# A two-layer gated block on one core: keys and values of the first cross-attention as one-pass products of high and low parts, the context transposed two steps sooner, loads in halves, the first statistics early

## What is computed

```python
ln = layer_norm(layernorm(x), gamma_l, beta_l)      # 112 latents for each of 8 batches
xn = layer_norm(ctx, gamma_x, beta_x)               # 375 context rows
q  = (ln @ Wq)                                      # 8 heads of 64
k_x, v_x = split(xn @ Wkv); k_l, v_l = split(ln @ Wkv)
k  = concat(rope(k_x), k_l); v = concat(v_x, v_l)   # 487 keys and values
x  = x + tanh(g) * (softmax(q k^T / 8) v) @ Wo
...                                                 # experts (top 2 of 8, and a shared one), then the
...                                                 # second layer's attention and expert attention
```

## Time and profile before

| | |
|---|---|
| median of 3 runs | 807.23 us (804.37 to 810.54) |
| profiled execution | 806.53 us |
| its span, first to last instruction | 804.7 us |
| TensorE / VectorE / ScalarE / GpSimd busy | 93% / 55% / 46% / 23% |
| mean granted TensorE clock | 0.994 of full speed |
| the stage in question | from the start to about 268 us |

### The profile page before, as it was taken

How to read it: one execution, slowest core, us unless ns; L and a number is a source line. 1 busy time by engine, 2 the same in 40 slices (tenths; PEclk the granted TensorE clock), 3 DMA queues, 4 the chain that set the end, 5 groups by cost and what they waited for, 6 DMA issues and landing times.

```text
span 804.7 us, 14480 instructions
## 1 busy us (share of the span) xinstructions
PE 752.2 (93%) x5152; PEld 553.4 (69%) x5152; DVE 446.2 (55%) x1136; ACT 371.8 (46%) x991; POOL 182.4 (23%) x301
## 2 busy tenths in 40 slices
PE   3889999999999999999999999998999988999998
PEld 1355555555564666698889888666676767889976
DVE  1657758667666331122122221857788788698741
ACT  2456656556565621132332232467787878211210
POOL 2212112112100026000000001754446535411000
PEclk9999999999999999899999999999999999999999
DMA  4422224233121394155645542260000000000001
GB/s 137 113 56 60 73 78 149 68 113 83 36 55 38 94 353 179 61 173 212 228 163 175 187 139 84 73 220 2 2 2 2 2 2 2 1 1 1 0 12 35
DMA packets 43451, 69.74 MB, mean 87 GB/s; under 512 B 6531, under 2 KB 34956, under 8 KB 43124
## 3 DMA queue, kind: packets, MB, share of 16 engines
q1 hardware_dynamic: 41844, 65.14, 25.4%
q0 software_dynamic: 1536, 3.67, 1.5%
HBM read 52.56 MB, written 8.26 MB: 76 GB/s over the span
## 4 chain that ended last, share of the span: by engine, by line
PE 73%; DVE 9%; DMA 6%; ACT 5%; issue 4%; POOL 2%; SPq 1%; ACTq 0%; DVEq 0%
PE ps L1362 10%; PE ps L1595 7%; PE ps L1607 7%; PE ps L1813 7%; PE ps L1406 6%; PE ps L1409 6%; DMA OT<-slot_rows 4%; PE ps L1526 4%; PE ps L1850 3%; PE ps L1448 3%; PE ps L1695 3%; PE ps L1515 3%; PE ps L1468 3%; PE ps L1396 2%; PE ps L1419 2%
## 5 line engine op out<-in xcount | busy, mean ns | idle before, releaser
L1362 PE MATMUL ps<-ident,arena 112*122 112x112 f32 (+5 forms) x584 | 82.9, 276 | 21.2 <-ACT arena L576 13.7
L732 ACT ACTIVATE OT<-ps,bt 128x128 f32<-128x128 f32 x168 | 47.9, 368 | 114.2 <-PE ps L1595 113.3
L1362 PEld LDWEIGHTS ps<-ident,arena 112*122 112x122 f32 (+5 forms) x584 | 63.8, 155 | 46.1 <-issue 27.7
L1595 PE MATMUL ps<-OT,arena 128*128 128x128 f32 x672 | 80.5, 279 | 0.2 <-DVE OT L1076 0.2
L1595 PEld LDWEIGHTS ps<-OT,arena 128*128 128x128 f32 x672 | 78.7, 196 | 0.6 <-issue 0.6
L927 DVE TENSOR_REDUCE negmax<-ps 112x1 f32<-112x375 f32 x128 | 61.1, 539 | 30.4 <-PE ps L1695 30.3
L1813 PE MATMUL ps<-arena_r 128*112 128x384 f32 x384 | 75.9, 346 | 1.9 <-DVE acc L1164 1.0
L1607 PE MATMUL ps<-arena,OT 128*128 128x256 f32 x336 | 75.8, 379 | 0.0
L922 DVE TENSOR_REDUCE negmax<-ps 112x1 f32<-112x487 f32 x64 | 39.4, 657 | 56.8 <-PE ps L1448 56.6
L1090 DVE COPY yo<-ps 128x256 f32<-128x256 f32 x21 | 8.9, 424 | 108.3 <-PE ps L1607 108.3
L1607 PEld LDWEIGHTS ps<-arena,OT 128*128 128x128 f32 x336 | 62.3, 190 | 7.6
(11 more groups left out here) (269 smaller groups left out, 1373.6 us busy)
## 6 DMA issues: line engine op xcount, KB each, us to landing
arena<-in_up_w SPq DMA_DIRECT2D x21, 1024.0 KB, 5.1
arena<-in_down_w SPq DMA_DIRECT2D x8, 1024.0 KB, 11.9
arena<-arena SPq DMA_DIRECT2D x128, 60.9 KB, 2.0
arena<-in_wqkv SPq DMA_DIRECT2D x1, 3072.0 KB, 10.4
arena<-in_ctx SPq DMA_DIRECT2D x8, 375.0 KB
slot_rows<-acc SPq DMA_DIRECT2D x3, 896.0 KB, 5.0
OT<-slot_rows SPq DMA_DIRECT2D x21, 128.0 KB, 5.0
slot_out<-yo SPq DMA_DIRECT2D x21, 128.0 KB, 1.7
```

The lines of the kernel that those rows point to most:

```text
L732: act.activation(he[:, i % 2, m, :], ps[:, 2 * (i % 2) + m // 4, (m % 4) * SLOT:(m % 4 + 1) * SLOT], ACT.Gelu, bias=bt[:, i % 3, m:m + 1]) ...
L1362: return pe.transpose(dst, src, ident[0:k, 0:k])
L1595: ins = pe.matmul(ps[:, 2 * (i % 2) + m // 4, (m % 4) * SLOT:(m % 4 + 1) * SLOT], wu[i % 3][:, c, m * P:(m + 1) * P], xgT[:, i % 2, c, :], ...
```

## The change

Six things, in the order of the diff's importance:

1. For batches 1 to 7 ScalarE makes `kv_hi`, the high part of `kvin` (`kv_high`, 128 x 976 elements, at the head of step 2 of the batch before), and VectorE `kv_lo` (`kv_low`, behind the two maxima of that step). The weights `wkv` are split once: `wkv_hi` by ScalarE ahead of the first keys (128 x 2048), `wkv_lo` by VectorE in two halves of 1024 at the ends of steps 0 and 1 of batch 0. `l0_kv` then makes each piece of six fp32r products in place of two fp32 ones (four records); TensorE waits for `kv_lo` first. Batch 0 stays in fp32. The two buffers are single.
2. `l0_t1` of batch n+1 moves from step 2 to step 0 (step 1 for n = 0), on TensorE behind the scores, on ScalarE ahead of the exponentials; `l0_q` moves from step 2 to the end of step 1. `ctx_hat(n + 2)` moves from step 3 to step 2. `L0_SEQ` follows.
3. The context of batch 1 is loaded ahead of the first swap; its statistics, and those of latents 1, are made before the first rotation; `hat` of batch 1 is made between the first two copies of keys. From then on the latents' statistics run two batches ahead in place of one.
4. The clearing DMAs of the experts' slots go in six halves of 448 KB in place of three of 896 KB; the shared expert's weights in four halves of 512 KB in place of two of 1024 KB; two loads of second-layer weights start two swaps later.
5. GpSimd's order follows VectorE's.
6. The arena grows by 256 columns (1 KB for each partition).

```diff
+        (kv_hi, kv_lo, wkv_hi, wkv_lo) = layout(21760, [P, KC, NKP0], [P, KC, NKP0], [P, KC, 1024], [P, KC, 1024], of=arena_r)
...
             sp.dma_start(x[:, 1, :], a["x"][1, :, :]).then_inc(s_x, 16)
+            ctx_load(1, cx, 1)
...
-                sp.dma_start(xs[k * B * TQ:(k + 1) * B * TQ, :].rearrange("(t p) d -> p t d", p=TQ), acc[:, :, :])\
+                half = B * TQ // 2
+                sp.dma_start(xs[k * half:(k + 1) * half, :].rearrange("(t p) d -> p t d", p=TQ), acc[:, 0:B // 2, :])\
...
-                    if i == 0:
-                        ctx_load(1, cx, 1)
...
-                    if i in (11, 15, 19):
-                        clear_slots(i // 4 - 2)
-                    if i == 14:
-                        sp.dma_start(sw_u, a["sw_up"].rearrange("(c p) n -> p c n", p=P)).then_inc(s_shw, 16)
-                    if i == 18:
-                        sp.dma_start(sw_d, a["sw_down"].rearrange("(m p) n -> p m n", p=P)).then_inc(s_shw, 16)
-                    if i == 22:
+                    if i in (11, 15, 16, 20, 22, 23):
+                        clear_slots((11, 15, 16, 20, 22, 23).index(i))
+                    if i in (12, 14):
+                        c = (12, 14).index(i)
+                        sp.dma_start(sw_u[:, c], a["sw_up"][c * P:(c + 1) * P, :]).then_inc(s_shw, 16)
+                    if i in (18, 19):
+                        m4 = (18, 19).index(i) * 4
+                        sp.dma_start(sw_d[:, m4:m4 + 4], a["sw_down"][m4 * P:(m4 + 4) * P, :]
+                                     .rearrange("(m p) n -> p m n", p=P)).then_inc(s_shw, 16)
+                    if i == 24:
...
-                    if c == 0 and n >= 2:
-                        act.wait_ge(L0["v"], (n - 1) * 4)
+                    if c == 0 and n == 2:
+                        act.wait_ge(L0["v"], 4)
+                    elif c == 0 and n > 2:
+                        act.wait_ge(s_kvlo, n)
...
+            def kv_high(n):
+                if n >= 2:
+                    act.wait_ge(L0["v"], 4 * n)
+                act.wait_ge(L0["t1e"], (n + 1) * KC)
+                act.activation(kv_hi, kvin[n % 2], ACT.Copy).then_inc(s_kvhi, 1)
...
+                if n + 1 < B and u == (n == 0):
+                    l0_t1(n + 1, q)
+                if n + 1 < B and u == 2:
+                    kv_high(n + 1)
                 l0_exp(n, 2 * u)
                 if u == 2:
-                    if n + 1 < B:
-                        l0_t1(n + 1, q)
...
-                    if u == 2:
-                        l0_q(n + 1, q)
...
+                if n + 1 < B and u == 1:
+                    l0_q(n + 1, q)
...
-                if n == 0 and u == 1:
-                    ctx_hat(1, 1)
-                if n + 2 < B and u == 3:
+                if n + 2 < B and u == 2:
                     ctx_hat(n + 2, p)
...
+            act.wait_ge(s_w0, 16)
+            act.activation(wkv_hi, wkv, ACT.Copy).then_inc(s_kvhi, 1)
             l0_k(0, 0)
             l0_q(0, 0)
             l0_v(0, 0, 0)
+            ctx_hat(1, 1)
...
+            dve.wait_ge(s_x, 16)
+            latents_stats(1, x, 0)
+            ctx_stats(1, 1)
+            latents_stats(1, xn, 1)
...
+            def kv_low(n):
+                if n >= 2:
+                    dve.wait_ge(L0["v"], 4 * n)
+                dve.wait_ge(s_kvhi, n + 1)
+                dve.tensor_tensor(kv_lo, kvin[n % 2], kv_hi.bitcast(F32), ALU.subtract).then_inc(s_kvlo, 1)
+
+            def w_low0(c):
+                dve.wait_ge(s_kvhi, 1)
+                dve.tensor_tensor(wkv_lo[:, c, :], wkv[:, c, :], wkv_hi[:, c, :].bitcast(F32), ALU.subtract)\
+                   .then_inc(s_kvlo, 1)
...
+                if n + 1 < B and u == 2:
+                    kv_low(n + 1)
+                if n + 2 < B and u == (2 if n == 0 else 0):
...
+                    latents_norm(1)
+                if n + 2 < B and u == (2 if n == 0 else 0):
+                    latents_norm(n + 2)
+                if n == 0 and u < 2:
+                    w_low0(u)
...
             def l0_kv(n, p, j, kinds=("k", "v")):
-                pe.wait_ge(L0["t1e"], (n + 1) * KC)
+                if n:
+                    pe.wait_ge(s_kvlo, 2 + n)
+                else:
+                    pe.wait_ge(L0["t1e"], KC)
                 for kind in kinds:
                     bank = l0_bank_free(kind, n, j)
                     for c in range(KC):
-                        if kind == "k":
+                        first, last = c == 0, c == KC - 1
+                        if n == 0 and kind == "k":
                             ins = pe.matmul(ps[:, bank, 0:NK0], wkv[:, c, j * P:(j + 1) * P], kvin[p][:, c, 0:NK0],
-                                            start=(c == 0), stop=(c == KC - 1))
+                                            start=first, stop=last)
+                        elif n == 0:
+                            ins = pe.matmul(ps[0:KP0, bank, :], kvin[p][:, c, j * KP0:(j + 1) * KP0],
+                                            wkv[:, c, 512:1024], start=first, stop=last)
                         else:
-                            ins = pe.matmul(ps[0:KP0, bank, :], kvin[p][:, c, j * KP0:(j + 1) * KP0],
-                                            wkv[:, c, 512:1024], start=(c == 0), stop=(c == KC - 1))
+                            for k, (wv, xv) in enumerate(((wkv_hi, kv_hi), (wkv_hi, kv_lo), (wkv_lo, kv_hi))):
+                                if kind == "k":
+                                    ins = pe.matmul(ps[:, bank, 0:NKP0], wv[:, c, j * P:(j + 1) * P], xv[:, c, :],
+                                                    start=first and k == 0, stop=last and k == 2)
+                                else:
+                                    ins = pe.matmul(ps[0:KP0, bank, :], xv[:, c, j * KP0:(j + 1) * KP0],
+                                                    wv[:, c, 512:1024], start=first and k == 0, stop=last and k == 2)
                     ins.then_inc(L0[kind], 1)
...
-                if u == 2 and n + 1 < B:
+                if n + 1 < B and u == (n == 0):
                     l0_t1(n + 1, q)
...
-                elif n + 1 < B:
-                    if u == 2:
-                        l0_q(n + 1, q)
+                if n >= 2 and u == 1:
+                    l0_x(n - 2)
+                if n + 1 < B and u == 1:
+                    l0_q(n + 1, q)
                 if n >= 2 and u == 2:
                     l0_r(n - 2)
                 if u >= 2 and n + 1 < B:
                     l0_kv(n + 1, q, u - 2)
-                if n >= 2 and u == 1:
-                    l0_x(n - 2)
 
...
+    def context(n):
+        return ("t1", n, 0), ("t1", n, 1)
 
     def pair(n, j):
         return ("k", n, j), ("v", n, j)
 
-    seq.extend(prelude() + pair(0, 1))
+    seq.extend(context(0) + (("k", 0, 0), ("q", 0, 0), ("v", 0, 0)) + pair(0, 1))
     for n in range(B):
-        seq.extend(pair(n, 2) + pair(n, 3))
+        if 0 < n < B - 1:
+            seq.extend(context(n + 1))
+        seq.extend(pair(n, 2))
+        if n == 0:
+            seq.extend(context(1))
+        seq.extend(pair(n, 3))
         if n >= 2:
             seq.append(("x", n - 2, 0))
         if n + 1 < B:
-            seq.extend(begin(n + 1))
+            seq.append(("q", n + 1, 0))
         if n >= 2:
             seq.append(("r", n - 2, 0))
         if n + 1 < B:
```

39 lines of the change are left out of this document (17 added, 22 removed).

## The result

The changed kernel takes **786.31 us** (median of four, 783.97 to 788.33) against 806.51 beside it (median of four, 804.37 to 810.54): a ratio of 0.975, 95% interval 0.9714 to 0.9785. The prediction said 782, in a range of 774 to 791. The profiled execution took 783.97 us, its span is 782.2; that of before took 806.5 with a span of 804.7. Two traces further down, of the changed kernel again and of the whole loads, are of executions 1.5% and more above the fastest run of their kernel, and their experts' loops count in no mean.

What follows compares the result with a forecast made beforehand. The first stage was taken as bound by TensorE's own pieces plus a little waiting. Terms 18.8 + 1.5 + 5.0 = 25.3 us off the profiled 806.5 gave 781.2, so 782 us as median, range 774 to 791.

Steps and rivals of the forecast that it cites:

- keys and values, 28 pairs: First stage, batches 1 to 7: six fp32r products replace four fp32 records; a pair 2.70 us against 3.37, 18.8 us off.
- waits of batches 1 to 6, net: Batches 1 to 6: queries' 4.5 us of waits go, 3.0 of new waits for kv_lo come; 1.5 us off.
- batch 0, beyond its pairs: Batch 0: scores of batch 1 begin at 52.6 us, not 59.0; 5.0 us off besides 1.3 in products.
- batch 7, beyond its pairs: Batch 7: no l0_t1 and no split, last steps hang on the rotation as before; 0 us.
- The rival of the streaming price: Keys and values: 15 ns overhead belongs to 112-column loads; a pair costs 2.55 us, total 778 or 775; chance 0.14.
- Uncovered weight loads: Keys and values: each weight load runs before its product, 0.1275 us each; a pair 4.03 us, total 819; chance 0.03.
- The wait for the low part: Step 2, batches 1 to 6: next batch's keys wait for VectorE's kv_lo, 0.5 us a batch, paid in full.
- VectorE as the pace: First stage: split on VectorE costs 1.2 us more where TensorE waits, seven times, 8.4 us; total 790; chance 0.12.
- last sign of being wrong: First stage: the prediction is wrong if scores start to wait for rotations; no size given.
- After 268 us nothing is changed: After the first stage: only the arena's end changes; expert loads are released by the same semaphores and move along.
- The rival "given back": After the stage: experts' weights or something else bound by a fixed time, so the end stays at 805; chance 0.03.

Runs made afterwards that it cites:

- second experiment: Changed kernel with the four products that need no low part first in each piece of keys and values: 783.36 us, ratio 0.9676 to the kernel before.
- seventh: Changed kernel with VectorE making the low part twice in a row: 805.28 us, ratio 0.9927 to the kernel before.
- ninth experiments: Changed kernel with the products that need no low part first and the low part made twice: 788.14 us, ratio 0.9757 to the kernel before.
- tenth experiment: Changed kernel with the first statistics and hat of batch 1 back in step 0 of batch 0, early context load kept: 793.44 us, ratio 0.9813.
- fourth experiment: Changed kernel with transposes and queries back in step 2, ctx_hat in step 3; split (moved to match) and early statistics kept: 809.97 us, ratio 0.9935.
- sixth kernel: Changed kernel with only the halving of the DMAs undone, whole clearing and weight loads at their old places: 790.15 us, ratio 0.9732 to the kernel before.
- the eighth: Changed kernel with the old order (transposes and queries in step 2), but ScalarE's scaling ahead of that step's first exponential: 796.53 us, ratio 0.9838.
- fifth kernel: Changed kernel with all splits and waits kept, but keys and values as fp32 products: 799.28 us, ratio 0.9873 to the kernel before.

## Why the prediction was right, step by step

At the end of the stage, profile against profile:

| step of the prediction | predicted, us | measured, us |
|---|---|---|
| keys and values, 28 pairs | 18.8 | 28 x 0.64 = 17.9 |
| waits of batches 1 to 6, net | 1.5 | 4.5 - 2.1 = 2.4 |
| batch 0, beyond its pairs | 5.0 | 32.5 - 25.2 - 1.3 = 6.0 |
| batch 7, beyond its pairs | 0 | -1.0 |
| sum | 25.3 | 25.3 (25.7 read directly) |

That the sums agree to 0.4 us is in part luck. The four terms are off by 0.9 to 1.0 us each, two of them up and two down, and what they leave out after the stage is larger than any.

**Keys and values.** The mechanism is the one forecast; the pair is 2.73 and not 2.70. The price per product, 0.223 us for 488 columns and 0.232 for 512, is the proportion to the 384-column row within 0.002, nearer than the sum with a constant that I took. The rival of the streaming price (2.55 a pair) is ruled out: the excess over one pass at 2.4 GHz is 18 to 20 ns a product here, not less than the 15 of the earlier trace rows. So the Trainium skill's N / 2.4 + 2.5 ns ("TensorE: Matmul & The Clock Gate", "Back-to-back issue gap", where it is called the isolated gap, without a budget for weight loads), by which, an estimate, the stage would have got some 6 us more, fails in this trace too.

**Uncovered weight loads.** Six products with full-height weights of 128 columns run in 1.34 us, though each load shows 188 ns in the rows of the tile; loads and products overlap. The prediction's 0.1275 us for an uncovered load was read off queries behind a wait; without one they take 1.79 us, 0.112 each. The sentence of "The mechanism" in the same page of the Trainium skill, by which loads overlap only where the row group differs, is contradicted; the section's other sentence, by which a load into a background weight buffer is pulled ahead too, would allow what the rows show.

**The wait for the low part.** Forecast 0.5 a batch, measured 0.35, and 0.8 in batch 0. Taking it away (second experiment) gives 3.2 us back, so it was on the path as said.

**VectorE as the pace.** The subtraction costs 1.165 us against the 1.18 forecast, so writing fp32r has no price, and VectorE has 5.3 us a batch to spare, as forecast. But the rival was nearer than its chance of 0.12 tells: with 1.2 us more in that place the kernel is at 805, not at 790. I had priced a wait at its length alone; the runs showed that behind a long one the clock comes on top (seventh and ninth experiments).

**Batch 0.** The forecast 6.4 us with its pairs came out as 7.3. The tenth experiment shows that, in the new order, it hangs on the early statistics: without them 7.0 of it are lost.

**Not foreseen.** In batch 7 the scores wait 1.9 us for rotations, where they waited 1.2: shorter pieces make the swap's landing the next limit, and 1.0 us of batch 7's own 1.3 is given back. It was the prediction's own last sign of being wrong that scores start to wait for rotations; in this one batch they already did, and now do so for longer. And the order was treated as worth 1.5 us net plus batch 0; the fourth experiment shows that with the order of before most of what the split saves is lost again to waits and clock.

**"After 268 us nothing is changed".** This is the sentence that failed, in part. The stage gave 25.7 us against a sum of 25.3, and yet the profiled execution missed 781.2 by 2.8 us and the median 782 by 4.3. The experts' loop took 3.2 us more in that execution and 3.7 more on the mean of seven. The rival "given back" had it as all or nothing, through loads tied to a fixed time; it is a seventh of the gain in the stage, through gathers and the clock around their waits, and its cause stays open. That the medians' distance is made there is worked out from profiled executions; the others have no trace.

## What to carry to other kernels

When TensorE's pieces get shorter, look at every wait that ends with another engine's work at a fixed pace: its length grows by what the piece has lost. Price such a wait twice, as its length and, from about 1.4 us on in this kernel, as the pieces behind it at half the clock in most cases; then move the producer ahead, or put first the products that don't need it, which here hid 0.9 us of wait at no cost. And when a gain is missing, set the stages of several traces side by side: one stage here seems to give back a part of what another had earned, and only a column of fourteen numbers showed it.

## What the hardware showed beyond that

- **Length of a wait and the clock.** In the fourteen traces, from 24 us to the stage's end, no wait of TensorE up to 1.34 us had a fall of the granted clock in it or right behind it; of the 24 waits from 1.39 us up 18 had one, 6 not, and there was no fall without such a wait. The shortest with a fall was 1.39 (batch 7 of the sixth kernel), the longest without 1.94 (in the eighth, where it fell after 1.83). What decides between a fall and none is open. The level that it falls to is 1.2 GHz, half of full speed: the slow stretch of the kernel before, traced again, has (length, busy PE, granted clock, DMA share, GB/s)

```profile
201.00:207.00 6.00, 6.00 (x19) 0.50 0.00 0
```

- **It shows in the spread.** The fourth kernel's twelve runs had mean granted clocks of 0.975 to 0.989 and times of 813.8 down to 798.3 us, the highest clocks with the lowest times.
- **An earlier stage's products and a later stage's gathers.** Only the type of the products differs between the fifth kernel and the changed one, and the loop that follows 80 us later takes 159.6 in one trace of the former and 162.9 and 168.8 in two of the latter. With the one fp32r trace that has 159.1 this is an observation, no cause.
- **fp32r products** cost 0.223 us for 488 columns (weights of 128 columns) and 0.232 for 512 (weights of 122): three such products in the place of one fp32 product (0.825 and 0.86 us) save 19%.
